# Segment sums of a gated attention: one matmul of depth 128 against running sums with matmuls of depth 8 in row groups of TensorE

## The chip, the cores and the metric

One core of a Trainium2 chip runs the whole kernel. The metric is the device time of one launch in microseconds (us). TensorE (PE in the profile; PEld is its weight load) multiplies into PSUM, VectorE (DVE), ScalarE (ACT) and GpSimd (POOL) do the element-wise work, SyncE (SP) issues the DMA transfers.

## The reference

The reference is a decoder on x of 4 x 512 x 128 (batch, sequence, model): a gated linear attention with 16 heads of 64, then a cross attention over 32 context rows, then six layers of windowed attention and feed-forward, with a layer norm behind each of the three parts. The change touches only the first part:

```python
log_alpha = -jax.nn.softplus(jnp.einsum('bsm,mh->bsh', x, Wa) + ba)
cum = jnp.cumsum(log_alpha, axis=1).transpose(0, 2, 1)
diff = cum[:, :, :, None] - cum[:, :, None, :]
decay = jnp.exp(jnp.where(causal, diff, -jnp.inf))
attn = jnp.einsum('bhid,bhjd->bhij', q, k) * decay
o = jnp.einsum('bhij,bhjd->bhid', attn, v)
```

So the pair of positions i and j of one head needs exp of the sum of log_alpha over the positions behind j up to i.

## The kernel before, in words

The sequence runs in 16 chunks of 128 positions, four in each of the four batches (chunk k = 4b + n). For each batch TensorE first makes 24 projections of 128 x 512 (`attn_project`, L414: eight for q, eight for k, eight for the gate), which ACT activates (L749) out of four PSUM banks. Among them stand the group norm's matmuls of the batch before (L418, L422) and its output projection (L428). Then come the four chunks. All engines have fixed queues, written out by hand; they meet only through semaphores.

One chunk on TensorE, in order:

- `segments(k, 0)`: for PSUM banks 0 and 1 (four heads of 128 x 128 pairs in each) a bfloat16 matmul (L439) that writes the causal mask (0 or a large negative number) and a float32 matmul (L440) that adds the segment sums. Its weights are the triangle t > j; its moving operand, 128 x 512, is log_alpha(t, head) times the triangle t <= i. POOL builds that operand for all 16 heads once a chunk (L1237, 128 x 2048), after both halves of the chunk before have read it.
- L463: the values of the chunk, to banks 4 and 5.
- `segments(k, 1)`: the same for banks 2 and 3.
- L472 (n < 3): transposes of the keys. L478 (n > 0): running sums per head, broadcast to the head's 64 rows. L449: the scores q k, half by half, into banks 0 to 3, after ACT has taken the exponential of the sums (L761). L490 (n > 0): the part that comes from the state. L496: scores times values. L503 (n < 3): the update of the state.

DVE in a chunk: keys times decay (L1044, behind L472), queries times decay (L1048, behind ACT's L781, which follows L478), scores times decay (L1053, twice), the state (L1056 to L1062) and batch-norm statistics (L1067, eight). At the start of a batch DVE aggregates the statistics of the one before (L1073) and passes them to L418.

A float32 matmul shows as two MATMUL records in the profile (two passes), a bfloat16 one as one. A tile form such as 128*128 gives the rows and columns of the array that a matmul uses; 64*128 in two different halves of the partitions are two row groups.

The numbers before and after: BATCHES = 4, so `rank_sum`, `rank` and the like of the change run four times, `segments` 32 times. SP loads seven small tensors into `attn_small_loaded` before the first projection weight (L307, L308).

Of the kernel before, what the change touches and what calls it, by code (L numbers as in the profile page):

```python
# [4 lines left out]
ALU = mybir.AluOpType  # L5
ACT = mybir.ActivationFunctionType
AX = mybir.AxisListType.X
PARTS = 128
# [21 lines left out]
def decoder(nc, io, LAYERS=6):  # L30
# [10 lines left out]
    SEQ = 512  # L41
# [4 lines left out]
    def sb(name, shape):  # L46
        return nc.alloc_sbuf_tensor(name, shape, F32)
# [13 lines left out]
    centre_w = sb('centre_w', [PARTS, PARTS])  # L61
    window_mask = sb('mask', [PARTS, 2, 64])
    tiny = sb('tiny', [PARTS, 2])
    arena = sb('work', [PARTS, 32000])
    cv = carver(arena)
    squares = cv(2, 1024)
    cos_part = cv(2, 1024)
# [32 lines left out]
    gate_act = av(8, SEQ)  # L100
    attn_heads = av(8, SEQ)
    v_chunk = av(1024)
    seg_operand = av(16, 128)
    pair_decay = av(16, 128)
    pair_scores = av(16, 128)
    head_decay = av(8, 128)
# [17 lines left out]
    ones = av(128)  # L124
# [162 lines left out]
    values_copied = nc.alloc_semaphore('values_copied')  # L287
    windows_loaded = nc.alloc_semaphore('windows_loaded')
    mask_ready = nc.alloc_semaphore('mask_ready')
    HIDDEN_CHUNKS = [128, 128, 85]  # L290

    def upto_all(count):
# [8 lines left out]
    with nc.Block() as block:  # L301

        @block.sync
        def _(sp):
            sp.dma_start(x_all[:, :], io['x']).then_inc(x_loaded, 16)
            for t, k in ((triangles, 'tri'), (w_alpha, 'a_wa'), (b_alpha, 'a_ba'), (ones, 'ones'), (ctx_t, 'ctx'), (w_cross, 'x_w'), (b_cross, 'x_b')):
# [76 lines left out]
        def _(pe):  # L383
# [10 lines left out]

            def attn_setup():
                pe.wait_ge(x_loaded, 16)
                pe.wait_ge(attn_small_loaded, 16 * 7)
# [26 lines left out]
            def attn_output(b, c):  # L424
# [4 lines left out]
                if c == 7:  # L429
                    m.then_inc(attn_out, 1)  # L430

            def segments(k, half):
                n = k % 4
                if n == 0:
                    pe.wait_ge(attn_activated, 6 * k + 22 + 2 * half)
                else:
                    pe.wait_ge(chunk_scores_decayed, 2 * k - 1 + half)
                for j in (2 * half, 2 * half + 1):
                    mm(psum[:, j, :], ident_bf16[:, :], causal_bf16_mask[:, :].unsqueeze(1).broadcast_to([PARTS, 4, 128]), start=True, stop=False)  # L439
                    m = mm(psum[:, j, :], triangles[:, 1, :], seg_operand[:, 4 * j:4 * j + 4, :], start=False, stop=True)  # L440
                m.then_inc(segment_sums, 1)

            def pair_products(k, half):
# [62 lines left out]
            def attention():  # L506
                attn_setup()
                pe.wait_ge(log_alpha_ready, 1)
                mm(psum[:, 5, 0:256], triangles[:, 1, :], log_alpha, start=True, stop=True).then_inc(tail_sums, 1)
                pe.wait_ge(ctx_copied, 3)  # L510
                for b in range(BATCHES):
                    for t in range(16):
                        if b == 0 and t == 0:
                            pe.wait_ge(attn_wq_loaded, 16)
                        if b == 0 and t == 8:
                            pe.wait_ge(attn_wk_loaded, 16)
                        if b and t == 8:
                            group_mean(b - 1)
                        if b and t == 12:
                            group_variance(b - 1)  # L520
                        attn_project(b, t)
                    if b == 0:
                        pe.wait_ge(attn_wg_loaded, 16)
                        pe.wait_ge(norm_consts_loaded, 16 * 3)
                        pe.wait_ge(attn_wv_loaded, 16)
                        pe.wait_ge(attn_wo_loaded, 16)
                    for c in range(8):
                        if b:
                            attn_output(b - 1, c)
# [415 lines left out]
        def _(dve):  # L945
# [90 lines left out]
            def chunk(b, n):  # L1036
# [30 lines left out]
                    m = V.bn_stats(chan_stats[:, c, 6 * n:6 * n + 6], attn_heads[:, c, nn])  # L1067
                m.then_inc(norm_stats, 1)

            def group_scales(b):  # L1070
                dve.wait_ge(norm_stats, 4 * b + 4)
                for c in range(8):
# [30 lines left out]
                V.tensor_tensor(xb, xb, psum[:, 7, :], ALU.add).then_inc(x_plus_out, 1)  # L1103

            def attention():
                dve.wait_ge(attn_small_loaded, 16 * 7)
# [10 lines left out]
                dve.wait_ge(norm_consts_loaded, 16 * 3)  # L1117
                V.tensor_copy(ident_bf16[:, :], ident[:, :]).then_inc(causal_bf16, 1)
                for b in range(BATCHES):
                    if b:  # L1120
                        group_scales(b - 1)
                        group_affine(b - 1)
                        gate_heads(b - 1)
                        add_output(b - 1)
                    for n in range(4):
                        chunk(b, n)
# [59 lines left out]
        def _(pool):  # L1186
# [45 lines left out]
            def attention():  # L1232
                pool.wait_ge(log_alpha_ready, 1)
                for k in range(16):
                    if k:
                        pool.wait_ge(segment_sums, 2 * k)
                    U.tensor_tensor(seg_operand, triangles[:, 0, :].unsqueeze(1).broadcast_to([PARTS, 16, 128]), log_alpha[:, k * 16:k * 16 + 16].unsqueeze(2).broadcast_to([PARTS, 16, 128]), ALU.mult).then_inc(segment_operand, 1)  # L1237
            pool.wait_ge(x_loaded, 16)
            pool.wait_ge(zeroed, 6)
            pool.wait_ge(attn_small_loaded, 16 * 7)  # L1240
            attention()
            stage(0, 0)
            pool.wait_ge(block_shifted, 2)
# [9 lines left out]
def shape_constants():  # L1253
# [20 lines left out]
    m0[0:32, 0:32] = -1e+30  # L1274
    a = np.arange(128)
    tri = np.stack([a[:, None] <= a[None, :], a[:, None] > a[None, :]], 1).astype(np.float32)
    bd = (a[:, None] // 64 == a[None, :] // 64).astype(np.float32) / 64
    return dict(base=rotary_base, mask=np.stack([m0, m1], 1).copy(), ident=np.eye(128, dtype=np.float32), mean_w=np.full((128, 128), 1 / 128, np.float32), centre_w=(np.eye(128) - 1 / 128).astype(np.float32), tri=tri, bd=bd, ones=np.ones((128, 128), np.float32))

def layout(a, LAYERS=6):  # L1280
    layer_vecs = np.zeros((128, LAYERS, 9), np.float32)
# [28 lines left out]
```

## Time and profile before

| | |
|---|---|
| median of 3 runs | 2317.48 us (2315.33 to 2319.54) |
| the profiled execution | 2324.95 us |
| its span, first to last instruction | 2323.2 us |
| busy: PE, DVE, ACT, POOL | 90%, 62%, 56%, 48% |
| mean granted clock of TensorE | 0.959 |
| the gated attention | about 20 to 382 us of the span |
| L440 (segment sums) | 128 passes, 592 ns each |
| L1237 (their operand, POOL) | 16, 3608 ns each |

Busy shares are means over stages. The record of a pass holds a tail of about 0.16 us behind its last column in which the next pass already runs, so the spacing of starts, not the length of a record, is what a pass costs. The clock is given as a share of 2.4 GHz; it has two levels, 1.00 and 0.50.

### The profile page before, as it was taken

Reading aid. Unit: us, or ns where it says so; the run is one execution under the profiler, and the core shown is the slowest. Engines: PE = TensorE matmul, PEld = TensorE weight load, DVE = VectorE, ACT = ScalarE, POOL = GpSimd, SP = SyncE. Lnnn points to the kernel's source line nnn. Section 1 sums busy time; section 2 is a strip of 40 time slices with the busy share of each in tenths; the row PEclk is TensorE's granted clock in tenths of the full one; section 3 lists DMA queues with packets and bytes.
Section 4 is the critical chain, followed back from the end, with each engine's and each line's share of the span. In section 5 each row is a group of like instructions: output and inputs, shape, how many; then the busy total and the mean of one; then the engine's idle time right before and its main releaser. Section 6 shows DMA issues by size and latency. Waiting matters only on the chain.

```text
span 2323.2 us, 75905 instructions
## 1 busy us (share of the span) xinstructions
PE 2096.4 (90%) x33992; PEld 1366.7 (59%) x33992; DVE 1434.9 (62%) x1552; ACT 1291.2 (56%) x1616; POOL 1122.8 (48%) x704
## 2 busy tenths in 40 slices
PE   8999998799999899999999899999999999999975
PEld 4655655366666566666665566666666666566651
DVE  1344444577766667677666676676766766676632
ACT  4444254355656666566556565665656655666552
POOL 1110210376655555556555565555555655556520
PEclk9999999799999999999999999999999999999995
DMA  3000000022223222232222332222222232222210
GB/s 101 1 1 1 2 19 28 17 59 59 73 58 83 71 60 57 57 84 67 72 58 57 78 81 64 51 63 75 75 65 56 61 80 68 68 62 65 56 38 18
DMA packets 81775, 128.17 MB, mean 55 GB/s; under 512 B 17070, under 2 KB 27948, under 8 KB 81324
## 3 DMA queue, kind: packets, MB, share of 16 engines
q1 hardware_dynamic: 81452, 123.32, 20.9%
q8 instruction: 269, 4.41, 0.9%
q14 instruction: 54, 0.44, 0.1%
HBM read 21.55 MB, written 1.05 MB: 10 GB/s over the span
## 4 chain that ended last, share of the span: by engine, by line
PE 62%; issue 13%; DVE 12%; ACT 11%; POOL 1%; DMA 0%; SPq 0%; POOLq 0%; ACTq 0%; DVEq 0%
PE ps L588 11%; PE ps L592 9%; PE ps L699 5%; PE ps L660 4%; PE ps L709 4%; PE ps L414 4%; DVE SS L995 4%; PE ps L668 3%; PE ps L597 3%; PE ps L598 3%; PE ps L634 3%; PE ps L440 2%; DVE work L964 2%; DVE MX L1010 2%; ACT work L876 2%
## 5 line engine op out<-in xcount | busy, mean ns | idle before, releaser
L960 DVE TENSOR_TENSOR work<-ps,work 128x1024 f32<-128x1024 f32 x192 | 235.2, 1225 | 388.9 <-ACT work L871 281.4
L1213 POOL TENSOR_TENSOR work<-work,RL 128x1024 f32<-128x1024 f32 x96 | 182.6, 1902 | 604.5 <-DVE RL L980 604.5
L592 PEld LDWEIGHTS ps<-ident,work 128*128 128x128 f32 x3072 | 350.9, 143 | 182.9 <-issue 153.6
L592 PE MATMUL ps<-ident,work 128*128 128x128 f32 x3072 | 394.3, 277 | 40.9 <-ACT work L876 20.8
L1231 POOL TENSOR_TENSOR work<-work,RS 128x1024 f32<-128x1024 f32 x192 | 361.1, 1902 | 116.3 <-ACT RS L924 116.3
L964 DVE TENSOR_TENSOR work<-ps,work 128x1024 f32<-128x1024 f32 x192 | 233.3, 1215 | 0.0
L1225 POOL TENSOR_TENSOR work<-work 128x1024 f32<-128x1024 f32 x96 | 226.6, 2360 | 13.2 <-DVE work L964 5.9
L1218 POOL TENSOR_TENSOR work<-work 128x1024 f32<-128x1024 f32 x96 | 227.6, 2371 | 4.5 <-DVE work L964 4.5
L588 PE MATMUL ps<-WQ,XS 128*128 128x512 f32 x384 | 216.5, 691 | 11.4 <-POOL XS L1203 4.0
L699 PE MATMUL ps<-work,WO 128*128 128x128 f32 x1536 | 204.6, 283 | 17.4 <-issue 15.6
L995 DVE TENSOR_REDUCE SS<-work 128x32 f32<-128x2048 f32 x96 | 218.5, 2276 | 0.0
L699 PEld LDWEIGHTS ps<-work,WO 128*128 128x128 f32 x1536 | 186.8, 193 | 32.9 <-issue 28.1
L1237 POOL TENSOR_TENSOR work<-work 128x2048 f32<-128x2048 f32 x16 | 57.7, 3608 | 301.4 <-PE ps L440 284.5
L709 PE MATMUL ps<-work 64*32 64x64 f32 x12288 | 161.1, 226 | 41.1 <-issue 40.9
L588 PE MATMUL ps<-WK,XS 128*128 128x512 f32 x384 | 185.4, 605 | 0.0
L660 PE MATMUL ps<-WV,XS 128*128 128x512 f32 x384 | 180.7, 592 | 0.5 <-ACT KT L894 0.5
L709 PEld LDWEIGHTS ps<-work 64*32 64x32 f32 x12288 | 139.1, 105 | 59.0 <-issue 45.3
L934 ACT ACTIVATE work<-ps 128x1024 f32<-128x1024 f32 x96 | 97.8, 1019 | 116.1 <-PE ps L709 116.0
L917 ACT ACTIVATE work<-ps 128x1024 f32<-128x1024 f32 x96 | 97.8, 1019 | 95.9 <-PE ps L592 95.6
L668 PEld LDWEIGHTS ps<-KT,work 64*32 64x32 f32 x12288 | 126.9, 105 | 40.7 <-issue 40.7
L871 ACT ACTIVATE work<-ps 128x1024 f32<-128x1024 f32 x96 | 98.5, 1026 | 93.8 <-PE ps L588 93.3
L668 PE MATMUL ps<-KT,work 64*32 64x64 f32 x12288 | 142.4, 225 | 0.0
(180 smaller groups left out, 3283.3 us busy)
## 6 DMA issues: line engine op xcount, KB each, us to landing
work<-work SPq DMA_DIRECT2D x576, 128.0 KB
work<-work SPq DMA_DIRECT2D x336, 64.0 KB
WQ<-in_wqkv SPq DMA_DIRECT2D x6, 512.0 KB, 3.8
WK<-in_wqkv SPq DMA_DIRECT2D x6, 512.0 KB, 3.9
WV<-in_wqkv SPq DMA_DIRECT2D x6, 512.0 KB, 3.7
WO<-in_wo SPq DMA_DIRECT2D x6, 512.0 KB, 3.9
work<-ZR SPq DMA_DIRECT2D x48, 64.0 KB
W<-in_w SPq DMA_DIRECT2D x6, 341.0 KB, 4.0
```

The costliest lines, as they stand in the source:

```text
L588: return mm(R[:, half, :], x_shift[:, 32 + at * 128:160 + at * 128], w[:, half * 512:half * 512 + 512], start=True, stop=True)
L592: m = nc.tensor.transpose(flat(R)[:, t * 128:t * 128 + 128], src[:, t * 128:t * 128 + 128], ident[:, :])
L660: m = mm(bank_x[:, q, :].rearrange('p (c d) -> p c d', d=64), x_shift[:, 32 + nb * 128:160 + nb * 128], w_v[:, :].rearrange('p (c q d) -> ...
L668: m = mm(bank_y[32 * w:32 * w + 32, q, c8 * 64:c8 * 64 + 64], q_t[64 * q:64 * q + 64, c8, 32 * w:32 * w + 32], k_t[64 * q:64 * q + 64, c8, ...
L699: m = mm(bank_f[:, 0, 0:128], w_o[:, k, :], heads_t[:, k, :], start=k == 0, stop=k == 7)
L709: m = mm(bank_z[32 * w:32 * w + 32, q, c8 * 64:c8 * 64 + 64], probs_t[64 * q:64 * q + 64, c8, 32 * w:32 * w + 32], v_win[64 * q:64 * q + 6 ...
L960: V.tensor_tensor(h16(cos_part[:, j, :]), h16(flat(src)), rotary_tabs[:, bass.ds(g // 16 * 1024 + (8 * j + n) * 64, 64)].unsqueeze(1).broa ...
L964: V.tensor_tensor(halves(sin_part[:, j, :]), halves(flat(src))[:, :, ::-1, :], rotary_tabs[:, bass.ds(g // 16 * 1024 + (8 * j + 4 + n) * 6 ...
L995: V.tensor_reduce(sq_sums[:, :, :], squares[:, :, :].rearrange('p a (h d) -> p a h d', d=64), AX, ALU.add).then_inc(k_sums, 1)
L1218: U.tensor_tensor(cos_part[:, 0, :], cos_part[:, 0, :], sin_part[:, 0, :], ALU.add).then_inc(q_rotated, 1)
L1225: U.tensor_tensor(cos_part[:, 1, :], cos_part[:, 1, :], sin_part[:, 1, :], ALU.add).then_inc(k_rotated, 1)
L1231: U.tensor_tensor(h16(qk_norm[:, j, :]), h16(cos_part[:, j, :]), inv_norms[:, j, :].unsqueeze(2).broadcast_to([PARTS, 16, 64]), ALU.mult). ...
```

## The change

The sum over a segment is the difference of two running sums, cum(i) - cum(j). For four heads that is a product of depth 8: four rows of weights hold 1 and meet cum(i) of one head each, four rows hold -cum(j) and meet 1. The eight rows of bank j stand at partitions 32j to 32j+7, so that the four banks' matmuls use four different row groups of the array.

- TensorE, once a batch: `rank_sum` makes the running sums of the four chunks, 4 float32 matmuls of 128 x 128 weights and 128 columns, to bank 6. Batch 0: before the first projection. Later batches: before the fourth.
- POOL, once a batch: a copy `rank_spread` of 128 x 512, log_alpha repeated so that each head's sum comes out on its rows.
- DVE, once a batch: `rank`, two operations on 128 x 512 from PSUM, ahead of the group norm's aggregates: the rows for the operand and the weights.
- POOL, once a chunk: the operand is now 128 x 512 (it was 128 x 2048), in two buffers.
- TensorE, in each half of a chunk: the two masks first, then the two matmuls of depth 8 and 512 columns.
- SP: one more small load (`rank_consts`, 128 x 8), in front of the first projection's weights; `attn_small_loaded` counts to 8.

```diff
-                sp.dma_start(... (w_cross, 'x_w'), (b_cross, 'x_b')) ...
+                sp.dma_start(... (w_cross, 'x_w'), (b_cross, 'x_b'), (rank_consts, 'rank')) ...
...
+            def rank_sum(b):
+                if b:
+                    pe.wait_ge(chunk_out_copied, 4 * b)
+                pe.wait_ge(ranks_spread, b + 1)
+                for n in range(4):
+                    m = mm(psum[:, 6, n * 128:n * 128 + 128], rank_spread[:, n * 128:n * 128 + 128], triangles[:, 0, :], start=True, stop=True)
+                m.then_inc(rank_sums, 1)
...
             def segments(k, half):
                 n = k % 4
                 if n == 0:
+                    pe.wait_ge(ranks_ready, k // 2 + 2)
                     pe.wait_ge(attn_activated, 6 * k + 22 + 2 * half)
                 else:
                     pe.wait_ge(chunk_scores_decayed, 2 * k - 1 + half)
                 for j in (2 * half, 2 * half + 1):
                     mm(psum[:, j, :], ident_bf16[:, :], causal_bf16_mask[:, :].unsqueeze(1).broadcast_to([PARTS, 4, 128]), start=True, stop=False)
-                    m = mm(psum[:, j, :], triangles[:, 1, :], seg_operand[:, 4 * j:4 * j + 4, :], start=False, stop=True)
+
+                for j in (2 * half, 2 * half + 1):
+                    m = mm(psum[:, j, :], rank_weights[32 * j:32 * j + 8, n * 128:n * 128 + 128], rank_operand[32 * j:32 * j + 8, n % 2, :, :], start=False, stop=True)
                 m.then_inc(segment_sums, 1)
...
                 mm(psum[:, 5, 0:256], triangles[:, 1, :], log_alpha, start=True, stop=True).then_inc(tail_sums, 1)
+                rank_sum(0)
...
+                        if b and t == 3:
+                            rank_sum(b)
                         attn_project(b, t)
...
+            def rank(b):
+                dve.wait_ge(rank_sums, b + 1)
+                if b:
+                    dve.wait_ge(segment_operand, 4 * b)
+                    dve.wait_ge(segment_sums, 8 * b)
+                V.tensor_scalar(rank_rows, psum[:, 6, :], rank_consts[:, 4:5], rank_consts[:, 5:6], ALU.mult, ALU.add).then_inc(ranks_ready, 1)
+                V.tensor_scalar(rank_weights, psum[:, 6, :], rank_consts[:, 6:7], rank_consts[:, 7:8], ALU.mult, ALU.add).then_inc(ranks_ready, 1)
...
                 for b in range(BATCHES):
+                    rank(b)
                     if b:
                         group_scales(b - 1)
...
                 for k in range(16):
-                    if k:
-                        pool.wait_ge(segment_sums, 2 * k)
-                    U.tensor_tensor(seg_operand, triangles[:, 0, :].unsqueeze(1).broadcast_to([PARTS, 16, 128]), log_alpha[:, k * 16:k * 16 + 16].unsqueeze(2).broadcast_to([PARTS, 16, 128]), ALU.mult).then_inc(segment_operand, 1)
+                    if k % 4 == 0:
+                        if k:
+                            pool.wait_ge(rank_sums, k // 4)
+                        U.tensor_copy(rank_spread.rearrange('p (a s i) -> p a s i', s=8, i=4), log_alpha[:, k * 16:k * 16 + 64].rearrange('p (a i) -> p a i', i=4).unsqueeze(2).broadcast_to([PARTS, 16, 8, 4])).then_inc(ranks_spread, 1)
+                    pool.wait_ge(ranks_ready, k // 4 * 2 + 1)
+                    if k > 1:
+                        pool.wait_ge(segment_sums, 2 * k - 2)
+                    U.tensor_tensor(rank_operand[:, k % 2, :, :], rank_rows[:, k % 4 * 128:k % 4 * 128 + 128].unsqueeze(1).broadcast_to([PARTS, 4, 128]), rank_consts[:, 0:4].unsqueeze(2).broadcast_to([PARTS, 4, 128]), ALU.mult).then_inc(segment_operand, 1)
```

## Rows read from the trace of the kernel before

**Rows 1.** The page: the span, and busy time, share and instructions of each engine.

```profile
span 2323.2 us, 75905 instructions
...
PE 2096.4 (90%) x33992; PEld 1366.7 (59%) x33992; DVE 1434.9 (62%) x1552; ACT 1291.2 (56%) x1616; POOL 1122.8 (48%) x704
```

**Rows 2.** Windows: stretch, length, PE, PEld, DVE, ACT, POOL busy, clock, DMA.

```profile
166.38:182.90 16.52, 15.73 (x187) 11.66 (x184) 7.56 (x14) 5.11 (x6) 3.61 (x1) 1.00 0.01 2
103.98:136.30 32.32, 29.81 (x70) 13.23 (x70) 13.74 (x40) 19.61 (x30) 0.00 (x0) 0.95 0.00 0
198.17:230.00 31.83, 29.32 (x74) 13.24 (x73) 13.78 (x40) 20.53 (x32) 0.00 (x0) 1.00 0.00 1
```

**Rows 3.** Timeline of PE, one chunk: start us, length us, engine, line, operation.

```profile
166.38 0.39 PE L439 MATMUL ps<-mkb,ident_bf 128*128 128x512 bf16 x1
166.60 1.02 PE L440 MATMUL ps<-work 128*128 128x512 f32 x2
...
168.53 1.88 PE L463 MATMUL ps<-WV,X 128*128 128x512 f32 x4
170.25 0.38 PE L439 MATMUL ps<-mkb,ident_bf 128*128 128x512 bf16 x1
...
172.40 1.04 PE L472 MATMUL ps<-ident,work 128*128 128x128 f32 x8
173.37 1.97 PE L478 MATMUL ps<-work 128*64 128x128 f32 x32
175.26 2.06 PE L449 MATMUL ps<-work 64*128 64x128 f32 x32
177.76 0.40 PE L490 MATMUL ps<-work 64*64 64x128 f32 x3 [0.45 <-issue]
```

**Rows 4.** The chain of waits, a last chunk: start us, us, what.

```profile
191.03 1.03 ACT work L781
...
192.12 1.66 issue
193.78 2.35 DVE work L1053 x2
```

**Rows 5.** Timeline of PE, the cross attention that follows the stage.

```profile
406.34 1.12 PE L562 MATMUL ps<-work 1*128 1x512 f32 x2
407.39 6.02 PE L566 MATMUL ps<-work 128*128 128x32 f32 x32
...
419.22 2.09 PE L574 MATMUL ps<-work 32*128 32x512 f32 x8 [0.78 <-DVE work L1161]
```

**Rows 6.** One line's instructions, L1048: count, duration ns min/median/max.

```profile
L1048 DVE TENSOR_TENSOR work<-work x12: 1224/1226/1773, 65.6 to 377.2; 128x1024 f32<-128x1024 f32 x12
```

**Rows 7.** Timeline behind the segments of a last chunk.

```profile
189.17 3.61 POOL L1237 TENSOR_TENSOR work<-work 128x2048 f32<-128x2048 f32 x1 [12.92 <-PE ps L440]
```

**Rows 8.** Timeline, projections behind batch 1.

```profile
201.01 1.12 DVE L1073 BATCH_NORM_AGGREGATE work<-work 128x2 f32<-128x24 f32 x8
...
205.14 0.28 PE L418 MATMUL ps<-work 128*128 128x8 f32 x2
...
208.80 0.28 PE L422 MATMUL ps<-work 128*128 128x8 f32 x2
...
211.59 0.70 PE L414 MATMUL ps<-X,WK 128*128 128x512 f32 x1 [2.50 <-ACT work L749]
```

**Rows 9.** Timeline of the start.

```profile
4.22 0.43 SPq L307 DMA_DIRECT2D work<-in_x_b  x1
4.70 0.43 SPq L308 DMA_DIRECT2D WQ<-in_a_wq  x1
...
8.65 1.64 PE L399 MATMUL ps<-work,X 128*128 128x16 f32 x7 [8.65 <-DMA work<-in_x_b]
```

**Rows 10.** One line's instructions, L1237: duration ns min/median/max, first start us.

```profile
L1237 POOL TENSOR_TENSOR work<-work x16: 3606/3608/3611, 19.1 to 357.8; 128x2048 f32<-128x2048 f32 x16
```

**Rows 11.** The same of L414.

```profile
L414 PE MATMUL ps<-X,WQ x64: 592/592/1061, 20.0 to 297.3; 128*128 128x512 f32 x64
```

More of the change, by code:

```diff
@@ L63, in decoder @@
     tiny = sb('tiny', [PARTS, 2])
-    arena = sb('work', [PARTS, 32000])
+    arena = sb('work', [PARTS, 32200])
     cv = carver(arena)
@@ L102, in decoder @@
     v_chunk = av(1024)
-    seg_operand = av(16, 128)
+    rank_rows = av(SEQ)
+    rank_weights = av(SEQ)
+    rank_operand = av(2, 4, 128)
+    rank_consts = av(8)
+    rank_spread = av(SEQ)
     pair_decay = av(16, 128)
@@ L289, in decoder @@
     mask_ready = nc.alloc_semaphore('mask_ready')
+    rank_sums = nc.alloc_semaphore('rank_sums')
+    ranks_ready = nc.alloc_semaphore('ranks_ready')
+    ranks_spread = nc.alloc_semaphore('ranks_spread')
     HIDDEN_CHUNKS = [128, 128, 85]
@@ L305, in _ @@
             sp.dma_start(x_all[:, :], io['x']).then_inc(x_loaded, 16)
-            for t, k in ((triangles, 'tri'), (w_alpha, 'a_wa'), (b_alpha, 'a_ba'), (ones, 'ones'), (ctx_t, 'ctx'), (w_cross, 'x_w'), (b_cross, 'x_b')):
+            for t, k in ((triangles, 'tri'), (w_alpha, 'a_wa'), (b_alpha, 'a_ba'), (ones, 'ones'), (ctx_t, 'ctx'), (w_cross, 'x_w'), (b_cross, 'x_b'), (rank_consts, 'rank')):
                 sp.dma_start(t, io[k].rearrange('o h -> (o h)').partition_broadcast(PARTS) if k == 'a_ba' else io[k]).then_inc(attn_small_loaded, 16)
@@ L396, in attn_setup @@
                 pe.wait_ge(x_loaded, 16)
-                pe.wait_ge(attn_small_loaded, 16 * 7)
+                pe.wait_ge(attn_small_loaded, 16 * 8)
                 for k in range(16):
@@ L1105, in attention @@
             def attention():
-                dve.wait_ge(attn_small_loaded, 16 * 7)
+                dve.wait_ge(attn_small_loaded, 16 * 8)
                 V.tensor_scalar(causal_bf16_mask[:, :], triangles[:, 0, :], -1.0, 1e+30, ALU.add, ALU.mult).then_inc(causal_bf16, 1)
@@ L1234, in attention @@
                 for k in range(16):
-                    if k:
-                        pool.wait_ge(segment_sums, 2 * k)
-                    U.tensor_tensor(seg_operand, triangles[:, 0, :].unsqueeze(1).broadcast_to([PARTS, 16, 128]), log_alpha[:, k * 16:k * 16 + 16].unsqueeze(2).broadcast_to([PARTS, 16, 128]), ALU.mult).then_inc(segment_operand, 1)
+                    if k % 4 == 0:
[6 more added lines that the diff above has]
+                    U.tensor_tensor(rank_operand[:, k % 2, :, :], rank_rows[:, k % 4 * 128:k % 4 * 128 + 128].unsqueeze(1).broadcast_to([PARTS, 4, 128]), rank_consts[:, 0:4].unsqueeze(2).broadcast_to([PARTS, 4, 128]), ALU.mult).then_inc(segment_operand, 1)
             pool.wait_ge(x_loaded, 16)
             pool.wait_ge(zeroed, 6)
-            pool.wait_ge(attn_small_loaded, 16 * 7)
+            pool.wait_ge(attn_small_loaded, 16 * 8)
             attention()
@@ L1276, in shape_constants @@
     tri = np.stack([a[:, None] <= a[None, :], a[:, None] > a[None, :]], 1).astype(np.float32)
+    row = a % 32
+    rank = np.concatenate([(row[:, None] % 4 == np.arange(4)[None, :]) & (row[:, None] < 8), np.stack([row < 4, (row >= 4) & (row < 8), -1.0 * ((row >= 4) & (row < 8)), row < 4], 1)], 1).astype(np.float32)
     bd = (a[:, None] // 64 == a[None, :] // 64).astype(np.float32) / 64
-    return dict(base=rotary_base, mask=np.stack([m0, m1], 1).copy(), ident=np.eye(128, dtype=np.float32), mean_w=np.full((128, 128), 1 / 128, np.float32), centre_w=(np.eye(128) - 1 / 128).astype(np.float32), tri=tri, bd=bd, ones=np.ones((128, 128), np.float32))
+    return dict(base=rotary_base, mask=np.stack([m0, m1], 1).copy(), ident=np.eye(128, dtype=np.float32), mean_w=np.full((128, 128), 1 / 128, np.float32), centre_w=(np.eye(128) - 1 / 128).astype(np.float32), tri=tri, rank=rank, bd=bd, ones=np.ones((128, 128), np.float32))
 def layout(a, LAYERS=6):
```

## The prediction

> **What bounds the kernel now.** I read the page first: TensorE is busy 90% of the span [rows 1], and the change touches only the first stage, the gated attention, some 42 to 382 us of 2323. So the question is whether TensorE sets the end in that stage, and what its segment sums cost there. The windows by stage say that it nearly does: of the 16.52 us of a middle chunk TensorE is busy 15.73 (the first of the windows), at a granted clock of 1.00 (2.4 GHz) [rows 2]. The timeline of TensorE over one chunk [rows 3] then shows the sequence: two masks (L439) and two float32 segment matmuls (L440) in a half, the value projection L463, the second half, the transposes L472, the head sums L478, the scores L449, then a wait before L490 and, not shown, another one before L496. The chain of waits over a last chunk [rows 4] shows what lies between L478 and L496: ACT's exponential, a DVE product (L1048), two DVE products (L1053). None of that chain starts from anything but L478 (in a first chunk, which has no L478, DVE's chain starts from L472), and both follow the segment matmuls on TensorE without a wait, so a microsecond taken out of the segments moves the rest of the chunk forward by a microsecond. POOL's operand (3.6 us a chunk) is finished long before the next chunk asks for it; shortening it gives nothing by itself.
>
> **What one segment matmul costs.** In [rows 3] L439 starts at 166.38 and L440 at 166.60, so a bfloat16 mask takes 0.215 us of the array; the four passes of L463 take 170.25 - 168.53 = 1.72 us, 0.43 a pass, 0.86 a float32 matmul of 512 columns (two passes). A half is now 2 x (0.215 + 0.86) = 2.15 us; twice that and L463's 1.72 make the 6.02 us between 166.38 and 172.40. Nothing there is exposed: all are full-array matmuls and weights are loaded under the matmul ahead.
>
> Depth 8 alone saves nothing: L562 has one row of depth and 512 columns, and from its start to that of L566 it takes 1.05 us [rows 5], more than the 0.86 of depth 128. Any gain must come from two row groups working at once. Two rows of the trace show that they do. L449 is 32 passes of 128 columns in two groups of 64 rows, so 16 deep if they overlap. A pass of 128 columns takes (1.04 - 0.16)/8 = 0.11 us in L472 (0.16 is the tail behind the last start: a record of 0.59 for a pass of 0.43); one after the other 32 would take 3.5 us, and L449 took 2.06 [rows 3]. L574 is the form that the change brings, 32*128 tiles with 512 columns, four groups, eight passes: 2.09 us [rows 5] at the lower clock level (1.2 GHz), where one pass has twice 0.43 = 0.86; eight would need 6.9. The two passes of a float32 matmul stay one behind the other in their group, but the groups run side by side. So a pair takes 0.86 instead of 1.72: **0.86 saved per half, 1.72 per chunk**.
>
> **What a change of tile form costs.** L562 stands between full-array matmuls: 1.05 - 0.86 = 0.19 us for one change (a weight load that nothing covers, 0.11 by L472's pass of as many columns, and a gap of 0.08). L472 to L478 to L449 in [rows 3] agree: 173.37 to 175.26 is 1.89 for 16 x 0.11 = 1.74 of passes. I take 0.20 a change; the ends are 0.15 (that last difference) and 0.42, where the whole gain is gone (below). In a chunk with n below 3 each half now goes into row groups behind its two masks and out again ahead of L463 or L472: 4 changes, 0.80. With n = 3 the second half goes straight into L478, which has other tiles already: 3 changes, 0.60. Net per chunk 1.72 - 0.80 = 0.92 (12 chunks) and 1.72 - 0.60 = 1.12 (4 chunks): 11.0 + 4.5 = **15.5 us saved**. The masks of a half are now behind one another, at the same cost. Everything behind them is shifted, not stretched: ACT's copy of the values (1.03 us, as L781 in [rows 4]) still ends before the second half's sums come, 1.7 us behind L463.
>
> **POOL's operand.** 128x2048 in 3.61 us becomes 128x512, in proportion 0.9 us. It hides either way, with one exception: in the last chunk of a batch there are no transposes, so POOL (189.17 to 192.78) [rows 7] still works when L1048 starts at 192.09. L1048 has two SBUF operands and takes 1.77 us there instead of 1.23, and it is on the chain (the 1.66 of "issue" in [rows 4] is L1048). The median of L1048 is 1.226 and its maximum 1.773 [rows 6]; a last chunk is followed by an operand in three of four batches, so this is 3 x 0.547 = **1.6 us**. After the change POOL has nothing to do there at all (the operand for the next chunk waits for the next batch's rank rows), and I count it as gained. Should DVE be slow there for another reason, 0 is gained.
>
> **What is added.** (1) rank_sum, four float32 matmuls of 128 columns per batch: 8 passes of 0.11, 0.87 us as in L472. For batches 1 to 3 it stands behind the third projection. From 198.17 to 205.14 TensorE has eight projections in 6.97 us, 0.87 each, so no pause; its idle 2.5 us of this part come later, before 211.59 [rows 8], and hang on L422 by way of ACT, which loads its table behind the group's variance. Nothing absorbs it: 3 x 0.87. Its waits are met: chunk_out_copied comes about 1.2 us behind the last chunk (an ACT copy like L781), three projections take 2.6, and POOL's spread copy was done a batch half earlier. (2) In batch 0 it waits for POOL's spread copy, which starts where L1237 starts now, 19.1 [rows 10], and at L1237's 1.76 ns a column takes at most 0.9; TensorE gets there at 20.0 [rows 11]. 0 to 0.1 of wait and 0.87 of work: 0.9. (3) Two DVE operations on 128x512 from PSUM per batch, 0.6 each by L1053's 2.35 for two of 128x1024 [rows 4]. They are put ahead of the batch-norm aggregates. rank_sum would end near 201.7, DVE's pair near 203.1, the aggregates (1.12) near 204.2; the matmul that wants them, L418, then stands at 206.0. 1.8 us of cover, cost nothing; without it each microsecond late would be one on the path. (4) One more small DMA, ahead of the weight of the first projection. The issues on SP are 0.47 apart, and the first matmul waits for the last small load [rows 9]: 0.47, or 0 if landing and not issue sets it. The weight behind it is wanted only at 20. Sum of the additions: 2.6 + 0.9 + 0.5 = **4.0 us**.
>
> **The sum.** -15.5 - 1.6 + 4.0 = -13.1 us. The profiled execution took 2324.95 us (span 2323.2 and 1.75 around it) and would take 2311.9; it was 7.5 above the median of the three timed runs, so on the median 2317.48 I forecast **2304.4**.
>
> **Own spread.** The change of tile form at 0.15 gives 3 us more; the DVE term, the DMA term and rounding are worth 2. The clock: the stretch behind batch 0 had a mean clock of 0.95 and took 0.5 us longer than the same stretch behind batch 1 at 1.00 [rows 2], with the idle of 2.5 us in both; a shifted schedule can meet that drop in none or all three of them, and likewise the drops later in the kernel: some 3 us either way. So 2298 to 2310 if the mechanism is as I read it.
>
> **Rivals.**
> *The row groups do not overlap.* Then the change doesn't do what it says: the pair takes 1.72 as before and the 60 tile changes are paid, -13.1 + 27.5 = +14.4, 2332, slower. For it: eight rows a group and a matmul that accumulates on a full-array mask in the same bank are forms of which the trace has no example. Against it: L449 and L574, the latter with the same tile and columns. 6%.
> *Changes of tile form cost twice as much.* There are 12 x 4 + 4 x 3 = 60 of them; each 0.1 us more takes 6 us. At 0.42 the gain is gone. The masks just ahead are 512 columns wide, and if the array has to empty fully, the tail of 0.16 replaces the gap of 0.08: 0.08 x 60 = 4.8 us, 2309.2. Beyond that, for a wait of the accumulating bank, up to no change. For: no row shows the switch inside an accumulation in float32. Against: L562's row, whose bank L566 then adds to. 12%, of which a third near no change.
> *The second pass's weights are not loaded under the first.* Each of the 32 pairs would then show one more load, 0.11 us (by the pass of 128 columns): 3.5 us, 2307.9. The trace speaks against it: in L449 the second passes sit in the same row groups as the first, and 32 passes two abreast at 0.11 + 0.11 would take 3.5 us, not 2.06. 4%.
> This is the case by the Trainium skill, "TensorE: Matmul & The Clock Gate", Part 3 (The mechanism): weights are loaded under a running matmul only when the row group differs; by that rule 2307.9, by the row 2304.4, and L449 disagrees with it.
> *More is gained*, for example because ACT and DVE get ahead and the short waits before L490 and L496 shrink: up to 0.8 us in 11 chunks. Against: both waits hang on L478 and L449. 3%.
> The forecast keeps 75%.
>
> **Numbers.** A measurement of this kernel can tell about 0.2%, 4.6 us. Range: 2298 to 2312, which takes in the forecast's own spread, the rivals near 2308, and leaves out the serial case and the upper end of the tile changes. Faster by over 0.2% (below 2312.8): 0.88; within: 0.05; slower: 0.07.
>
> **What the profile after should show.** Rank matmuls in pairs starting within 10 ns, each pass 0.59 long, and 0.86 + 0.2 us between the end of the masks and L463's load; a middle chunk 15.6 us instead of 16.5, a last one 1.7 us shorter than now; L1048 never above 1.23; L1237's successor near 0.9; batches 1 to 3 with 0.87 more before L418; the first matmul at 9.1. Wrong would be: pairs one behind the other (serial), more than 0.3 us of nothing ahead of L463 (tile change), L418 waiting for DVE.

## The result, and the profile after

The changed kernel took 2297.82 us in the median of 17 runs (2291.35 to 2314.64); the kernel before took 2317.48 in 17 runs beside it. The ratio is 0.9919, with a 95% interval of 0.9903 to 0.9935: 18.8 us faster, between 15.1 and 22.5. The forecast was 13.1 us and 2304.4 us, with a range of 2298 to 2312. 2317.48 x 0.9919 is 2298.7, inside; the median itself lies 0.2 us below the lower end. The direction and the mechanism were right, the size was too small.

The page after, answering to [rows 1]:

```profile
span 2296.0 us, 76006 instructions
...
PE 2076.3 (90%) x34024; PEld 1352.0 (59%) x34024; DVE 1440.0 (63%) x1560; ACT 1291.3 (56%) x1616; POOL 1084.2 (47%) x708
```

The two profiled executions differ by 27.2 us in span, far more than the ratio. So I read stage by stage. Where the attention stage ends is seen at the start of the last chunk's "scores times values" (L496 before, L514 after), in the chain of waits of each. Before:

```profile
380.85 1.17 PE ps L496 x17
```

After:

```profile
366.49 1.98 PE ps L514 x32
```

The stage ends 14.4 us earlier, and this is what the forecast of 13.1 was made for. From the start of this line in the first chunk to its start in the last it is 314.00 us instead of 328.10, so 14.1, and two further traces of the changed kernel and one of the kernel before, all taken later, have the same two lengths; the remaining 0.3 lies in the start of the kernel, which differs from trace to trace. The other 12.8 us of this pair of traces, and the 4.4 us by which the ratio exceeds the stage, are the subject of the last experiments.

One middle chunk on TensorE after (timeline; start us, length us), answering to [rows 3]:

```profile
161.45 0.60 PE L455 MATMUL ps<-mkb,ident_bf 128*128 128x512 bf16 x2
161.99 1.13 PE L458 MATMUL ps<-work 8*128 8x512 f32 x4
163.04 1.98 PE L481 MATMUL ps<-WV,X 128*128 128x512 f32 x4
164.86 0.59 PE L455 MATMUL ps<-mkb,ident_bf 128*128 128x512 bf16 x2
165.39 1.13 PE L458 MATMUL ps<-work 8*128 8x512 f32 x4
166.45 1.09 PE L490 MATMUL ps<-ident,work 128*128 128x128 f32 x8
167.47 1.97 PE L496 MATMUL ps<-work 128*64 128x128 f32 x32
169.37 2.06 PE L467 MATMUL ps<-work 64*128 64x128 f32 x32
...
177.01 0.60 PE L455 MATMUL ps<-mkb,ident_bf 128*128 128x512 bf16 x2
```

The chunk runs from 161.45 to 177.01, 15.56 us instead of 16.52. L458 is the pair of depth-8 matmuls: four passes of 0.43 us each between 161.99 and 163.04, 1.05 us. That is two slots of 0.43, not four, and 0.19 of change of form (read as 0.11 for a weight load that nothing covers and 0.08 of gap). From the first mask to the transposes it is 166.45 - 161.45 = 5.00 us, where it was 6.02.

The last chunk of a batch in the changed kernel (the chain of waits; start us, us, what), answering to [rows 4]:

```profile
184.02 1.03 ACT work L802
...
185.11 1.11 issue
186.22 2.36 DVE work L1074 x2
```

One line's instructions in the changed kernel, L1069, which was L1048 (operation and count, shortest, median and longest instance in ns, first and last start in us, forms):

```profile
L1069 DVE TENSOR_TENSOR work<-work x12: 1225/1226/1227, 64.4 to 362.9; 128x1024 f32<-128x1024 f32 x12
```

The "issue" of 1.66 us is 1.11 now, and no instance of DVE's product is above 1.23 us, where the maximum was 1.77 [rows 6]. POOL's operand (L1273) takes 1.04 us, not the 0.9 that the prediction scaled.

The projections behind batch 1, answering to [rows 8] (timeline):

```profile
190.62 2.84 PE L421 MATMUL ps<-X,WQ 128*128 128x512 f32 x6
...
193.29 1.05 PE L444 MATMUL ps<-work 128*128 128x128 f32 x8
...
194.39 0.81 DVE L1097 TENSOR_SCALAR work<-ps,work 128x512 f32<-128x512 f32 x1 [0.96 <-PE ps L444]
...
195.83 1.11 DVE L1103 BATCH_NORM_AGGREGATE work<-work 128x2 f32<-128x24 f32 x8
...
198.48 0.28 PE L425 MATMUL ps<-work 128*128 128x8 f32 x2
...
202.14 0.28 PE L429 MATMUL ps<-work 128*128 128x8 f32 x2
...
204.93 0.30 PEld L421 LDWEIGHTS ps<-X,WK 128*128 128x128 f32 x2 [2.60 <-ACT work L770]
```

L444, the running sums, takes its 0.9 us between the third and the fourth projection. DVE's first of two operations starts behind it, and the aggregates (L1103) end at 196.94, 1.5 us before L425 wants them at 198.48. TensorE's 2.5 us of idle before 204.93 are what they were.

The start, answering to [rows 9]:

```profile
4.64 0.43 SPq L314 DMA_DIRECT2D work<-in_rank  x1
...
8.97 6.98 PE L406 MATMUL ps<-work,X 128*128 128x16 f32 x32 [8.97 <-DMA work<-in_rank]
...
19.46 0.61 POOL L1269 COPY work<-work 128x512 f32<-128x512 f32 x1 [17.19 <-DVE work L1146]
...
20.36 1.91 PE L444 MATMUL ps<-work 128*128 128x128 f32 x8
```

The first matmul waits for the added load and starts at 8.97 instead of 8.65. That is no measure of what the load costs: the same program, run again (`e4_after_again`), starts it earlier than the kernel before did.

```profile
8.14 6.98 PE L406 MATMUL ps<-work,X 128*128 128x16 f32 x32 [8.14 <-DMA work<-in_rank]
```

POOL's copy ends at 20.07, before L444 wants it at 20.36.

### The profile page after: what moved, and what is told of

Read it like the earlier page. It is cut to its first block, busy times and chain, and to the rows that moved or that the text cites. A ratio compares the mean times of both kernels' runs of the same rounds, so it can differ in the third digit from the quotient of the medians.

```text
span 2296.0 us, 76006 instructions
## 1 busy us (share of the span) xinstructions
PE 2076.3 (90%) x34024; PEld 1352.0 (59%) x34024; DVE 1440.0 (63%) x1560; ACT 1291.3 (56%) x1616; POOL 1084.2 (47%) x708
## 3 DMA queue, kind: packets, MB, share of 16 engines
HBM read 21.55 MB, written 1.05 MB: 10 GB/s over the span
## 4 chain that ended last, share of the span: by engine, by line
PE 60%; DVE 14%; issue 13%; ACT 12%; POOL 1%; DMA 0%; SPq 0%; POOLq 0%; ACTq 0%; DVEq 0%
PE ps L609 11%; PE ps L613 9%; PE ps L720 5%; PE ps L681 4%; DVE SS L1016 4%; PE ps L730 4%; PE ps L421 4%; PE ps L689 3%; PE ps L618 3%; PE ps L619 3%; PE ps L655 3%; DVE work L985 2%; DVE MX L1031 2%; ACT work L920 2%; ACT work L897 2%
## 5 line engine op out<-in xcount | busy, mean ns | idle before, releaser
L1273 POOL TENSOR_TENSOR work<-work 128x512 f32<-128x512 f32 x16 | 16.5, 1040 | 291.7 <-PE ps L458 160.9
L997 DVE TENSOR_REDUCE LE<-work 128x16 f32<-128x1024 f32 x96 | 116.9, 1217 | 42.3 <-ACT work L873 42.3
```

## The experiments

The first four kernels take the change apart, the next three carry it further, the last two ask where the rest of the measured gain comes from. Starts of L514 (or the line that stands for it) in successive chunks are used as the clock of a chunk: 16.53 us before and 15.56 after in a middle chunk, 16.20 and 14.54 in a last one (the distance from chunk 2 to chunk 3 of a batch).

**One row group for both.**

```diff
-                    m = mm(psum[:, j, :], rank_weights[32 * j:32 * j + 8, n * 128:n * 128 + 128], rank_operand[32 * j:32 * j + 8, n % 2, :, :], start=False, stop=True)
+                    m = mm(psum[:, j, :], rank_weights[64 * half:64 * half + 8, n * 128:n * 128 + 128], rank_operand[64 * half:64 * half + 8, n % 2, :, :], start=False, stop=True)
```

> The changed kernel, with both depth-8 matmuls of a half in one row group (that of the half's first bank), so that the second bank of each half gets the sums of the wrong four heads. Nothing else differs: masks first, two changes of tile form in a half. Theory (the gain is the overlap of two row groups): the four passes of a half stand one behind the other, 0.43 us each, 1.72 instead of 0.86 us, so a middle chunk grows from 15.56 to 17.3 us, and the stage by 32 x 0.86 = 27.5 us: the time comes out near 2325, 8 us above the kernel before. Rival (depth 8 is cheaper in itself, or the masks behind one another save something): the passes keep most of their gain, the chunk stays below 16.5 us and the time below 2317.

Median 2319.82 us (10 runs) beside 2313.05 for the kernel before (23 runs), ratio 1.0028 (1.0003 to 1.0053). The timeline of TensorE:

```profile
155.96 0.61 PE L455 MATMUL ps<-mkb,ident_bf 128*128 128x512 bf16 x2
156.50 1.98 PE L458 MATMUL ps<-work 8*128 8x512 f32 x4
158.41 1.98 PE L481 MATMUL ps<-WV,X 128*128 128x512 f32 x4
```

The four passes take 1.91 us instead of 1.05: 0.86 more, the slot that the overlap had saved. A middle chunk has 17.27 us, 1.71 above the changed kernel, which makes 16 x 1.71 = 27.4 for the stage, against the 27.5 expected. The stage itself ends 28.8 us later (at 395.30): this trace's clock was at its lower level from 51.4 to 54.8 us, in the first chunk. By the ratios on this chip the run is 25 us above the changed kernel and 6.5 us (0.7 to 12.3) above the kernel before, where 8 was expected. Matmuls of depth 8 in one row group are slower than the full-depth ones they replace: a middle chunk is 0.74 longer than the 16.53 of before, which is four changes of form. The whole gain is the overlap; depth alone is a loss.

**Mask and matmul taking turns.**

```diff
                 for j in (2 * half, 2 * half + 1):
                     mm(psum[:, j, :], ident_bf16[:, :], causal_bf16_mask[:, :].unsqueeze(1).broadcast_to([PARTS, 4, 128]), start=True, stop=False)
-
-                for j in (2 * half, 2 * half + 1):
                     m = mm(psum[:, j, :], rank_weights[32 * j:32 * j + 8, n * 128:n * 128 + 128], rank_operand[32 * j:32 * j + 8, n % 2, :, :], start=False, stop=True)
```

> The changed kernel with mask and depth-8 matmul taking turns, as in the kernel before (mask, matmul, mask, matmul in a half); each matmul keeps its own row group. Theory (a change of tile form costs 0.19 us and separates the groups): no overlap, 27.5 us, and two more changes in each of 32 halves, 64 x 0.19 = 12 us: some 39 us above the changed kernel, 2337, a middle chunk of 18.0 us. Rival (changes of form cost nothing, the array only waits for the weights): as the run with one row group, 2325. Rival (a mask in the whole array can run beside a row group): no change against the changed kernel.

Median 2341.94 us (4 runs), ratio 1.0136 (1.0096 to 1.0176). The timeline:

```profile
164.68 0.39 PE L455 MATMUL ps<-mkb,ident_bf 128*128 128x512 bf16 x1
165.00 1.12 PE L456 MATMUL ps<-work 8*128 8x512 f32 x2
166.05 0.39 PE L455 MATMUL ps<-mkb,ident_bf 128*128 128x512 bf16 x1
166.37 1.12 PE L456 MATMUL ps<-work 8*128 8x512 f32 x2
167.42 1.98 PE L479 MATMUL ps<-WV,X 128*128 128x512 f32 x4
...
173.04 3.54 PE L494 MATMUL ps<-work 128*64 128x128 f32 x32
```

A full-array mask between two row groups keeps them apart: each matmul takes 1.05 us by itself, so the order of the changed kernel, masks first, is part of what makes it faster. A middle chunk at the full clock has 17.86 us, 0.59 above the run with one row group, for four changes of form more: 0.15 each on average, not 0.19, since half of them go into a mask, whose bfloat16 weights load almost at once (1.37 from 165.00 to 166.37, less 0.86 of passes and 0.215 of mask, is 0.30 for the two changes, 0.19 and 0.11). The sum expected 39 us above the changed kernel; by the ratios it is 2341.9 - 2294.3 (the changed kernel, same chip, below) = 47.6. Part of the excess shows in the last line: L494, head sums that take 1.97 us, took 3.54 in this chunk, at the lower clock level, though the longest idle of TensorE in the 28 us ahead of it is 1.69 us. Nine of this trace's twelve distances between chunks of one batch are 0.8 to 2.9 us longer than at the full clock; in the changed kernel's trace none is. The profiled execution, 12 us above the median of the four, has 55 us at the lower level in the stage behind the clock's first rise, and the stage ends 59.6 us later than in the changed kernel: at the full clock all chunks together would give 16 x 2.30 = 36.8, near the sum. Why the clock falls here isn't shown.

**The kernel before with a small operand on POOL.**

```diff
-                    U.tensor_tensor(seg_operand, triangles[:, 0, :].unsqueeze(1).broadcast_to([PARTS, 16, 128]), log_alpha[:, k * 16:k * 16 + 16].unsqueeze(2).broadcast_to([PARTS, 16, 128]), ALU.mult).then_inc(segment_operand, 1)
+                    heads_made = 16 if k == 0 else 4
+                    U.tensor_tensor(seg_operand[:, 0:heads_made, :], triangles[:, 0, :].unsqueeze(1).broadcast_to([PARTS, heads_made, 128]), log_alpha[:, k * 16:k * 16 + heads_made].unsqueeze(2).broadcast_to([PARTS, heads_made, 128]), ALU.mult).then_inc(segment_operand, 1)
```

> The kernel before, with POOL writing only the first four of sixteen heads of the operand from chunk 1 on (0.9 us instead of 3.6); the other heads keep chunk 0's operand. TensorE's work is that of the kernel before. Theory (POOL's long operation slows L1048 in the last chunk of a batch): no L1048 above 1.23 us, and three last chunks are 0.55 us shorter: 1.6 us, which the timed runs cannot tell from no change and the trace can. Rival (L1048 is slow there for its place behind L449, or for what TensorE reads): three of twelve stay at 1.77 us.

One line's instructions in this kernel, first DVE's product:

```profile
L1048 DVE TENSOR_TENSOR work<-work x12: 1224/1226/1226, 66.9 to 376.5; 128x1024 f32<-128x1024 f32 x12
```

And POOL's operand, in the same view:

```profile
L1238 POOL TENSOR_TENSOR work<-work x16: 1039/1040/3607, 19.3 to 357.1; 128x512 f32<-128x512 f32 x15, 128x2048 f32<-128x2048 f32 x1
```

With the operation on POOL at 1.04 us instead of 3.61, all twelve of L1048 are at 1.23. TensorE's program is the same. A last chunk has 15.65 us instead of 16.20, 0.55 less, in the three batches that the prediction named; the kernel before has 15.65 too in the fourth, where no operand follows. So POOL's long operation slowed a DVE operation with two SBUF operands from 1.23 to 1.77 us, and that stood on the path. The timed runs: 2305.14 us (10 runs), ratio 0.9969 (0.9942 to 0.9997), 7.2 us where 1.6 was expected; see the control below.

**The changed kernel again.** No edit.

> The changed kernel, unchanged. The attention stage ends 14.4 us earlier than before in its trace, but its timed runs lie 18.8 us lower (15.1 to 22.5). Theory (the rest is where the clock fell to its lower level in the later stages, which differs from run to run): the stage again ends 14.4 us earlier, the ratio's interval reaches 0.9938 (14.4 us), and the later stages' length follows the time at the lower level, half a microsecond for one. Rival (the later stages are shorter for a lasting reason): at equal time at the lower level they are shorter than those of the kernel before by some 4 us.

Median 2294.31 us (6 runs) beside 2313.05, ratio 0.9920 (0.9891 to 0.9949). The last chunk's L514 starts at 366.77, 14.1 us before 380.85; the chunks have the same 15.56 and 14.54. So the stage's gain stands, and 14.4 us (0.9938) lies inside the interval. The later stages are not decided by this trace: from the first layer projection to the end it has 1866.2 us with 125.5 at the lower level, where the kernel before has 1888.6 with 163.6. With half a microsecond taken off for each one at the lower level, 1803.5 stands against 1806.7.

**All four row groups at once.**

```diff
-                segments(k, 0)
+                masks(k, 0)
+                if n:
+                    masks(k, 1)
...
-                segments(k, 1)
+                if n == 0:
+                    masks(k, 1)
+                segments(k)
```

`masks` holds the masks of a half and their waits, `segments` the four depth-8 matmuls of banks 0 to 3, one behind the other. On ACT, `pair_decays(k, 0)` moves behind the copy of the values.

> The changed kernel with all four depth-8 matmuls of a chunk together: masks of the four banks (for the first chunk of a batch the last two behind the values), the values, then the four matmuls in four row groups, then the transposes; ACT copies the values first and takes both exponentials behind. Theory (four groups run side by side as two do): a chunk saves one slot of 0.86 us and two changes of tile form, 0.86 + 0.37 = 1.23 us, so a middle chunk has 14.3 us instead of 15.56, the stage is 16 x 1.23 = 19.7 us shorter, at most 1.5 less for ACT's exponentials being late in first chunks: near 2279. Rival (only two groups run at once): the slot is not saved, 0.37 a chunk, 6 us, 2292. Rival (ACT's two exponentials behind one another become the wait ahead of L449): the chunk saves less than 0.6 us.

Median 2279.10 us (6 runs) beside 2313.83 (11 runs), ratio 0.9841 (0.9808 to 0.9875). The timeline:

```profile
154.26 1.04 PE L455 MATMUL ps<-mkb,ident_bf 128*128 128x512 bf16 x4
...
155.14 1.96 PE L486 MATMUL ps<-WV,X 128*128 128x512 f32 x4
...
157.03 1.14 PE L460 MATMUL ps<-work 8*128 8x512 f32 x8
157.13 1.02 ACT L797 ACTIVATE work<-ps 128x1024 f32<-128x1024 f32 x1 [2.67 <-PE ps L486]
...
158.10 1.10 PE L497 MATMUL ps<-ident,work 128*128 128x128 f32 x8
...
159.12 1.09 PE L503 MATMUL ps<-work 128*64 128x128 f32 x16
```

Eight passes of L460 take 158.10 - 157.03 = 1.07 us, as long as four did. A middle chunk has 14.40 us, 1.16 less than the changed kernel; 1.23 was expected. The difference: L486 now stands behind a wait for DVE's reading of the state bank, which is short, but leaves most of its first weight load uncovered (0.08 us: the first two passes of L486 start 0.51 apart, not 0.43). A last chunk saves 0.97, because the head sums (L503 of this kernel), which there stand right behind L460, wait 0.2 us for ACT's copy. The stage ends at 350.07, 16.4 before the changed kernel's; two of its batch changes (43.82 us where the third has 42.12) met the lower clock level, one of three in the changed kernel, which is 1.7 us. So 18.1 of the expected 19.7; 0.5 of it is not the edit's, for the first chunk comes 1.64 earlier and its own gain is 1.16.

**The running sums in TensorE's idle time.**

```diff
                         if b and t == 12:
                             group_variance(b - 1)
-                        if b and t == 3:
                             rank_sum(b)
```

On DVE, `rank(b)` moves behind `group_affine(b - 1)`.

> The changed kernel with the running sums of batches 1 to 3 moved on TensorE from ahead of the fourth projection to behind the group's variance, where TensorE waits 2.5 us for ACT's table, and DVE's two operations moved behind the group's affine. Theory (their 0.87 us a batch stood on the path and nothing absorbed them): the idle there shrinks from 2.5 to 1.6 us, the stage ends 3 x 0.87 = 2.6 us earlier. Rival (they were covered by another wait in the projections): no change in the stage. Rival (DVE's 1.2 us, now ahead of the gating, reach L435's wait): up to 1.2 us a batch lost again.

Median 2291.40 us (4 runs), ratio 0.9903 (0.9872 to 0.9935). The timeline:

```profile
198.64 0.28 PE L429 MATMUL ps<-work 128*128 128x8 f32 x2
...
198.78 1.14 PE L444 MATMUL ps<-work 128*128 128x128 f32 x8
...
200.91 2.22 POOL L1273 TENSOR_TENSOR work<-work 128x512 f32<-128x512 f32 x2 [50.80 <-DVE work L1096]
...
201.43 3.70 PE L421 MATMUL ps<-X,WK 128*128 128x512 f32 x8 [1.51 <-ACT work L769]
...
202.26 1.41 DVE L1127 TENSOR_TENSOR work<-work 128x512 f32<-128x512 f32 x1
```

The idle before L421 is 1.51 us instead of 2.51: the running sums now lie in it. From the last chunk's L514 to the first one of the next batch it is 42.34 us instead of 43.23 at the full clock, 0.89 a batch, 2.7 in the stage, as expected. The stage ends at 362.10, 4.4 us before the changed kernel's; the other 1.7 is a fall of the clock between batches 0 and 1 that the changed kernel's traces have (44.91 for 43.23) and this one hasn't. DVE's pair did not reach L435. The last line shows POOL once more: L1127, a product of two SBUF operands that takes 0.69 us otherwise, took 1.41 beside POOL's L1273.

**Both.** The edits of the last two.

> Both together. If the two gains are independent they add: 19.7 + 2.6 = 22 us below the changed kernel, 2276. Rival (they meet in one wait): less than the sum.

Median 2269.19 us (6 runs) beside 2313.83, ratio 0.9816 (0.9782 to 0.9851): 43 us below the kernel before, more than twice the gain of the change, and the fastest kernel here. The stage ends at 345.14, 21.35 before the changed kernel's, against the 22 expected, and 1.7 of this is again a fall of the clock that did not come. From the first chunk's L514 (or its successor) to the last's, the four groups save 16.55 us here beside the late sums and 16.50 in the run without them, clock drops taken off: the two gains are independent.

**A control, the kernel before timed as a variant.** No edit.

> A control: the kernel before, unchanged, timed as if it were the changed one. So far the timed runs of every variant, the one of the kernel before with POOL's small operand too, lie some 3 us lower against the kernel before than the attention stage in their traces says. Theory (that is how the comparison falls, for instance by the order in which the kernels run): this one comes out about 3 us lower than the kernel before as well, ratio near 0.9987. Rival (the variants gain those 3 us somewhere): ratio 1.000 within its interval.

Median 2307.14 us (12 runs) beside 2312.87 (21 runs), ratio 0.9980 (0.9954 to 1.0005). The same program came out 0.2%, 4.6 us, faster than itself. The interval just holds 1, so an order effect isn't shown; but of a ratio's last 0.2% nothing should be made here.

**The changed kernel with the layers put back to their old start.**

```diff
             cross()
+            for _ in range(21):
+                mm(psum[:, 0, :], mean_w[:, :], rotary_base[:, 0:2, :, :].rearrange('p a b c -> p (a b c)'), start=True, stop=True)
```

> The changed kernel with 21 more float32 matmuls of 512 columns (18 us at the full clock) on TensorE between the cross attention and the layers, whose result nobody reads, so that the layers start about where they start in the kernel before. Theory (the change gains 14.4 us in the attention and nothing else; the layers cost the same wherever they start): the time comes out 0 to 3 us beside the kernel before, as the filling puts the layers' start. Rival (something else of the changed kernel makes the layers shorter): with the layers starting at the same time as in the kernel before, 3 to 5 us below it.

Median 2304.91 us (10 runs), ratio 0.9964 (0.9943 to 0.9985): 8.3 us (3.5 to 13.2) below the kernel before. Read against the kernel before alone, this is the rival's sign and not the theory's. Read against the control, which ran on the same chip, it is 2.2 us lower in the median with intervals that overlap, and that decides nothing. Windows from the first layer projection to the end of the span (stretch, length, busy PE, PEld, DVE, ACT, POOL, clock, DMA). The kernel before:

```profile
434.63:2323.20 1888.57, 1712.81 (x31072) 1126.59 (x31072) 1263.86 (x1189) 1109.76 (x1380) 1062.68 (x676) 0.96 0.25 63
```

The control:

```profile
433.88:2305.30 1871.42, 1697.05 (x31072) 1121.82 (x31072) 1264.29 (x1189) 1109.61 (x1380) 1062.82 (x676) 0.97 0.26 64
```

This kernel:

```profile
435.87:2307.80 1871.93, 1699.49 (x31073) 1121.18 (x31071) 1263.43 (x1188) 1109.56 (x1380) 1060.20 (x675) 0.97 0.26 64
```

The changed kernel:

```profile
420.32:2296.00 1875.68, 1705.74 (x31072) 1125.12 (x31072) 1264.69 (x1189) 1109.43 (x1380) 1063.10 (x676) 0.96 0.26 64
```

Control and filled kernel have layers of 1871.4 and 1871.9 us, at the same clock. The two executions of the kernel before differ by 17.2 us in the same code, and the small-operand run, whose layers are the same code too, has 1855.9. So the layers' length varies by itself from run to run, with the share of time at the lower clock level: these three average 1872.0 us, and the three traces of the changed kernel's stage (1875.7, 1866.2, 1871.9) 1871.3. The traces don't show that the change or its earlier start shortens them; three of each can't exclude a few microseconds.

## Why the prediction was right, and where it was short

- **Only two groups at once bring the gain; 0.86 per half.** Right: the pair takes two slots of 0.43 us, one row group takes four (27.4 us in the stage against 27.5 worked out). L449 and L574 were the right rows to read it from, and L562 the right row for depth alone.
- **0.20 per change of form, 60 of them.** Measured 0.186 from the chunk (1.71 for the overlap, from the run with one row group, less 0.97 net, over four). So the net is 0.97 a chunk and 1.12 in a last one instead of 0.92 and 1.12: 12 x 0.97 + 4 x 1.12 = 16.1 us for 15.5. Had I kept the 0.19 of the L562 row instead of rounding it up, it would have been 16.
- **POOL and L1048, 1.6 us.** Right, and shown by the small-operand run: 0.55 in each of three chunks.
- **Running sums on the path, 0.87 in batches 1 to 3.** Right (0.89), and moving them out gave it back.
- **The start, 1.4 us.** Half wrong: the 0.87 of the running sums was right, and the 0.47 of the added load shows in no trace. One pair of traces misleads here. The first chunk's L514 starts 0.26 earlier than before (52.49 for 52.75), but this place moves with two things that differ from run to run: when the first matmul starts, and when the granted clock first rises from the lower to the full level (in the trace's record of the granted clock). Between the two TensorE works at half speed, so a microsecond later in either costs half a microsecond here:

| trace | first matmul | clock rises | first L496 or L514 | less half of both |
|---|---|---|---|---|
| before | 8.65 | 22.84 | 52.75 | 37.01 |
| before again | 8.30 | 21.96 | 52.14 | 37.01 |
| before, small operand | 8.81 | 25.13 | 53.98 | 37.01 |
| after | 8.97 | 22.20 | 52.49 | 36.90 |
| after again | 8.14 | 23.60 | 52.77 | 36.90 |
| after, filled | 8.70 | 24.13 | 53.31 | 36.89 |

  At an equal start the changed kernel is 0.11 earlier there: 0.97 from its own segments, less the running sums' 0.87. The first matmul of all eight kernels with the added load starts at 8.04 to 8.97 (mean 8.39), of the three without it at 8.30 to 8.81 (mean 8.59), so the prediction's other value for the load, 0, fits better.
- **The sum.** 16.1 + 1.6 - 3.5 (four times the 0.87 of the running sums) = 14.2 at an equal start, and the traces have 14.1 + 0.1; 13.1 was forecast. Of the 1.1 that it was short, 0.6 is the rounded change of form and 0.5 the load. The pair's 14.4 has another 0.15 from its start.
- **The clock in the spread.** The prediction put the fall of the clock behind batch 0 at 0.5 us, from two windows of [rows 2] that don't end at the same place: the second runs 1.14 us into the next chunk. From the last chunk's L496 to the next batch's first it is 45.01 against 43.31, so one such fall costs 1.7 us. The changed kernel's three traces have the same one, so it did not touch the result.
- **The rivals.** No overlap is excluded by the timeline; a second load per pair too: 1.05 us for L458 has room for 0.86 of passes, one load and one gap. The run with one row group says it more plainly: its four passes take 1.91 us, four slots and one change of form, so three of the four loads lay under passes of their own row group. By the Trainium skill, "TensorE: Matmul & The Clock Gate", Part 3 (The mechanism), weights are loaded under a running matmul only when the row group differs; these 1.91 us disagree with it. The same section also lets a load into the background weight buffer go ahead of running matmuls, and that would agree. A dearer change of form is excluded by the 0.186.
- **What is left, 4.4 us.** The ratio says 18.8 (15.1 to 22.5), the stage 14.4, and 13.1 lies below the interval too. The changed kernel timed again, against the kernel before on its chip, came out at 0.9920, with 14.4 us (0.9938) inside its interval; the control came out at 0.9980. All nine other comparisons, the control's included, lie 3.6 to 14 us lower than their traces' stages say (14 in the run whose clock fell so often, 9.5 in the filled one, by its layers' start). That speaks for the comparison rather than for the change: 0.9919 over the control's 0.9980 is 0.9939, or 14.1 us, with some 7 us either way. In the traces the layers are no shorter. I take the rest for the scatter of the layers' clock and of the comparison itself; that is argued, not shown. A gain of 14.2 alone would have given 2303.3, inside the range as well.

The forecast's own spread (2298 to 2310) named the clock as 3 us either way. The scatter of single runs, 2299 to 2322 for one program on one chip, was wider than that, and the one profiled execution from which I scaled was 7.5 us above its median.

## What to carry to other kernels

Here a matmul of small depth cost what a deep one costs, 0.43 us a pass; it pays only if several of them stand next to one another in different row groups, with nothing for the whole array between them, and each change of form must be paid from that (here 0.19 us against 0.43 us a pass). Count on both sides: with two at a time nearly half of the gain was eaten (0.74 of 1.71 us a chunk), with four at a time it more than doubled. Look for what a shorter operation on another engine frees: POOL's operand was hidden and yet held a DVE product back; and put new work where the engine already waits.

## What the runs showed of the hardware that was not expected

- With single depth-8 matmuls, each between masks, the clock was at its lower level in the middle of chunks (L494 3.54 us instead of 1.97), in nine of twelve chunk distances, with TensorE busy 52.7 of 56 us around there. With the same matmuls in pairs there was no such fall within a chunk, and with them behind one another in one group one, in the first chunk. It is one trace of each order (three of the pairs), and the cause is open.
- Going from a row-group matmul into a full-array bfloat16 one cost 0.11 us, going into a float32 one 0.19: the records of the weight loads behind the change differ by as much, 0.18 us for float32 and 0.10 for bfloat16.
- POOL's 128x512 product took 1.04 us, 0.29 of the 3.61 for four times the columns, and two of DVE's operations from PSUM with a scalar for each partition took 0.81 and 0.80 us where 0.6 was expected; all were hidden.
